# Four transformer layers on one core: order of work chosen per engine, other ranks, corrected costs, second batch begun later

## The reference

```
h = norm(x) * (1 + scale) + shift       # scale, shift, gate from the condition
x = x + gate * self_attention(h) @ Wo   # 16 heads of 16
x = x + gate * cross_attention(norm(x), context) @ Wco
x = x + gate * mlp(norm(x))             # 256 -> 1024 -> 256
```

## Time and profile before

| | |
|---|---|
| median of 3 runs | 3409.06 us (3408.49 to 3410.03) |
| profiled execution | 3412.44 us, span 3410.7 us |
| mean granted TensorE clock | 0.884 |
| TensorE busy | 2778.7 us |
| VectorE busy | 1942.9 us |
| ScalarE busy | 1529.7 us |
| POOL busy | 664.6 us |

### The profile page before, as it was taken

How to read it: one execution, slowest core, us unless ns; L and a number is a source line. 1 busy time by engine, 2 the same in 40 slices (tenths; PEclk the granted TensorE clock), 3 DMA queues, 4 the chain that set the end, 5 groups by cost and what they waited for, 6 DMA issues and landing times.

```text
span 3410.7 us, 44340 instructions
## 1 busy us (share of the span) xinstructions
PE 2778.7 (81%) x13323; PEld 1254.6 (37%) x13376; DVE 1942.9 (57%) x4404; ACT 1529.7 (45%) x2745; POOL 664.6 (19%) x970
## 2 busy tenths in 40 slices
PE   4899999888789898889777655785478989889777
PEld 3423343235325223243443434452223522323335
DVE  6785666332583776634444577338786278745141
ACT  2136546562444665645444223332244265655442
POOL 4011101201410111221141246212431001031020
PEclk8789999899789999989877767897589999999868
DMA  4511112311621322330553333322121031231140
GB/s 155 185 28 45 45 56 77 111 42 42 192 62 41 101 78 67 97 96 20 145 160 90 100 115 107 84 67 86 49 66 34 16 108 50 89 103 39 35 130 23
DMA packets 254273, 275.88 MB, mean 81 GB/s; under 512 B 60485, under 2 KB 195423, under 8 KB 253663
## 3 DMA queue, kind: packets, MB, share of 16 engines
q1 hardware_dynamic: 242783, 271.58, 27.0%
q0 software_dynamic: 11264, 1.46, 0.3%
HBM read 157.36 MB, written 114.09 MB: 80 GB/s over the span
## 4 chain that ended last, share of the span: by engine, by line
PE 62%; DVE 13%; DMA 8%; issue 7%; ACT 5%; POOL 2%; SPq 1%; ACTq 0%; DVEq 0%; POOLq 0%
PE ring_c L1267 10%; PE ring_a L1193 10%; PE ring_b L1237 8%; PE ring_b L1290 7%; PE ring_a L1302 6%; PE ring_b L1152 4%; PE ring_a L1279 3%; PE ring_b L1236 3%; ACT probs L1371 3%; DVE row_max L1533 3%; DMA reciprocals<-scr_recip 2%; PE ring_b L1118 2%; PE ring_a L1290 2%; PE ring_a L1166 1%; PE ring_b L1261 1%
## 5 line engine op out<-in xcount | busy, mean ns | idle before, releaser
L1371 ACT ACTIVATE probs<-ring_b 128x512 f32<-128x512 f32 (+1 forms) x1728 | 910.4, 601 | 691.6 <-PE ring_b L1237 596.1
L1533 DVE TENSOR_REDUCE row_max<-ring_a 128x1 f32<-128x1024 f32 x512 | 599.2, 1219 | 99.8 <-PE ring_a L1193 95.5
L1237 PE MATMUL ring_b<-q_ring,k_ring 100*128 100x512 bf16 x1536 | 525.8, 391 | 85.2 <-ACT probs L1371 61.0
L1193 PE MATMUL ring_a<-k_ring,q_ring 96*128 96x512 bf16 x1536 | 476.5, 403 | 36.1 <-DVE row_max L1533 21.6
L1267 PE MATMUL ring_c<-probs,v_and_ones 128*17 128x512 f32 x3072 | 420.0, 619 | 10.7 <-ACT probs L1371 7.4
L1651 POOL CAST neg_max_parts<-neg_max 16x128 bf16<-16x128 f32 x112 | 33.6, 300 | 1696.5 <-ACT neg_max L1365 1217.3
L1530 DVE CUSTOM_DVE_ANT_0 w_mlp<-ring_a,w_mlp 128x1024 bf16<-128x1024 f32 x256 | 301.3, 1222 | 87.1 <-PE ring_a L1193 86.1
L1577 DVE TENSOR_TENSOR x_tok<-x_tok,ring_a 128x512 f32<-128x512 f32 x96 | 66.0, 687 | 447.1 <-PE ring_a L1302 284.9
L1237 PEld LDWEIGHTS ring_b<-q_ring,k_ring 100*128 100x128 bf16 x1536 | 144.7, 99 | 374.0 <-issue 260.5
L1193 PEld LDWEIGHTS ring_a<-k_ring,q_ring 96*128 96x128 bf16 x1536 | 119.8, 100 | 402.3 <-issue 355.4
L1290 PE MATMUL ring_b<-h_feat,w_mlp 128*128 128x512 f32 x512 | 235.4, 610 | 4.2 <-ACT h_feat L1336 3.4
(11 more groups left out here) (138 smaller groups left out, 3390.2 us busy)
## 6 DMA issues: line engine op xcount, KB each, us to landing
q_ring<-scr_q SPq DMA_DIRECT2D x128, 384.0 KB, 4.0
scr_q<-split SPq DMA_DIRECT2D x64, 384.0 KB, 2.6
k_ring<-scr_k SPq DMA_DIRECT2D x64, 384.0 KB, 5.0
scr_q<-split SPq DMA_DIRECT2D x64, 256.0 KB, 3.0
scr_out<-out_stage SPq DMA_DIRECT2D x128, 128.0 KB, 2.9
scr_out<-out_stage SPq DMA_DIRECT2D x64, 256.0 KB, 2.8
h_feat<-scr_out SPq DMA_DIRECT2D x56, 256.0 KB
reciprocals<-scr_recip SPq DMA_DIRECT2D x56, 256.0 KB
```

What stands on the lines that cost most here:

```text
L1193: last = mm(ps[:, half * BLOCK:(half + 1) * BLOCK], q[0:PARTS, h, t * P:(t + 1) * P], k_view(g)[0:PARTS, h, half * BLOCK:(half + 1) * BLOC ...
L1237: last = mm(ps[:, :], k_view(g)[0:ROWS, h, s.kt * P:(s.kt + 1) * P], q[0:ROWS, h, q0:q0 + BLOCK], start=not g.masked, stop=True)
L1371: f(PT[0:n, s.pt, :], ps[0:n, :], ACT.Exp, **kw).then_inc(b_evac, 1)
L1533: v.tensor_reduce(NM[:, s.nm, s.u:s.u + 1], ps, AX.X, ALU.max).then_inc(a_evac, 1)
```

## The change

`run()` takes the step that can begin first (ties by rank), looks at the engine of its first phase, and picks by rank only among steps that begin on this engine, within a reach that depends on it: PE 0.25 us as before, ACT 5, DVE 0.8, POOL 0.15, SP 2. The ranks change: top-k to 0 and 1, the scores of cross-attention and the context's projections to 0, self-attention's scores to 5 beside its maxima, MLP and products with v to 6, cross maxima and all of window attention to 8. (`init` and `mod` of the table are used by no thread.) A new request `("many", pool, n, free)` takes n places at once when at least `free` are free; scores ask for four, the turns of top-k for two (with four free for the first pair of a unit). Some believed costs change, and the second batch's thread starts at 60 instead of 16 us of the planner's clock.

```diff
@@ -159,6 +159,16 @@
                     t.at = max(t.at, p.since[i])
                     p.uses[i] += 1
                     reply = (i, p.last[i], p.uses[i])
+                elif w[0] == "many":
+                    p = self.pools[w[1]]
+                    if len(p.free) < w[3]:
+                        return False
+                    reply = []
+                    for _ in range(w[2]):
+                        i = p.best()
+                        p.free.remove(i)
+                        t.at = max(t.at, p.since[i])
+                        reply.append((i, p.last[i]))
                 else:
                     if w[1] not in self.flags:
                         return False
@@ -199,8 +209,10 @@
             if not ready:
                 assert not self.threads, [(t.rank, t.send) for t in self.threads]
                 return self
-            first = min(at for at, _ in ready)
-            at, t = min(((at, t) for at, t in ready if at <= first + 0.25), key=lambda x: (x[1].rank, x[0]))
+            first, head = min(((at, t) for at, t in ready), key=lambda x: (x[0], x[1].rank))
+            eng = head.want["ph"][0][0]
+            at, t = min(((at, t) for at, t in ready if t.want["ph"][0][0] == eng and at <= first + REACH[eng]),
+                        key=lambda x: (x[1].rank, x[0]))
             s, t.want = t.want, None
             self.emit(s, at)
             t.at = max(t.at, s["t0"])
@@ -211,7 +223,9 @@
     return Step(kind=kind, ph=ph, after=list(after), counts=list(counts), **kw)
 
 
-RANK = dict(init=0, mod=2, prep=1, out=0, ctx=2, load=1, cross_f=3, cross_s=3, mlp=4, self_f=5, self_pv=5, self_s=6)
+RANK = dict(init=7, mod=0, prep=1, out=0, ctx=0, load=1, cross_f=8, cross_s=0, mlp=6, self_f=5, self_pv=6, self_s=5, tk=0, tk_s=1, win_f=8, win_s=8)
+REACH = dict(PE=0.25, ACT=5, DVE=0.8, POOL=0.15, SP=2)
+DELAY = [8.0, 60.0]
 
 
 def plan():
@@ -274,7 +288,7 @@
                      which=which, hh=hh, blk=blk, raw=raw, raw_last=raw_last, split=sp, sp_uses=sp_uses - 1, width=width,
                      rope=rope, h=h)
         p.raise_flag(("proj",) + key, s)
-        d = yield do("split", ([("PE", 1.0 * (0.6 if ck else 1))] if rope else []) + [("DVE", f * (4.4 if rope else 2.0) + 0.4)],
+        d = yield do("split", ([("PE", 1.0 * (0.6 if ck else 1))] if rope else []) + [("DVE", f * (4.4 if rope else 1.85))],
                      after=[s], ring="a" if rope else None, counts=["split_n"], of=s, rope=rope, l=l)
         p.give("RAW", raw, d)
         w = yield do("scratch", [("SP", 1.5)], after=[d], lat=3.5, of=s, done=d)
@@ -303,11 +317,11 @@
         p.spawn(projections(st, key, whiches), rank("prep"))
         p.spawn(loads(st, key, whiches), rank("load"))
         if topk:
-            p.spawn(topk_units(st, key), rank("cross_f"))
+            p.spawn(topk_units(st, key), rank("tk"))
         else:
-            p.spawn(firsts(st, key), rank("self_f" if kind == "full" else "cross_f"))
-            p.spawn(seconds(st, key), rank("self_s" if kind == "full" else "cross_s"))
-        p.spawn(products(st, key), rank("self_pv" if kind == "full" else "cross_s"))
+            p.spawn(firsts(st, key), rank({"full": "self_f", "window": "win_f", "cross": "cross_f"}[kind]))
+            p.spawn(seconds(st, key), rank({"full": "self_s", "window": "win_s", "cross": "cross_s"}[kind]))
+        p.spawn(products(st, key), rank({"full": "self_pv", "window": "win_s", "cross": "cross_s"}[kind]))
         for hh in range(KF):
             for n in range(hh * st.groups // KF, (hh + 1) * st.groups // KF):
                 yield ("flag", key + ("put", n))
@@ -431,7 +445,7 @@
             row = yield from row_load(l, 0, "vb")
         for blk in range(BLOCKS):
             h = yield ("flag", key + ("h", BLOCKS - 1 if st.akind == "window" else blk))
-            s = yield do("v", [("PE", 4.7), ("DVE", 1.8)], after=[h, w, last, row], ring="a", l=l, b=b, u=blk, last=last, row=row,
+            s = yield do("v", [("PE", 4.4), ("DVE", 1.5)], after=[h, w, last, row], ring="a", l=l, b=b, u=blk, last=last, row=row,
                          h=h)
         if row is not None:
             p.give("ROW", row.slot, s)
@@ -505,8 +519,8 @@
             g = s.g
             for kt in range(TILES if kind == "full" else 1):
                 unit = Step(g=g, kt=kt, last=kind != "full" or kt == TILES - 1, quarter=[], scores=[])
-                for tile in range(4):
-                    qt, pt_last, _ = yield ("get", "PT")
+                places = yield ("many", "PT", 4, 4)
+                for tile, (qt, pt_last) in enumerate(places):
                     pe = 0.43 if (kind == "full" and g.masked) else 0.45 if kind == "window" else 0.22
                     s = yield do("score", [("PE", pe), ("ACT", 0.6)], after=[g.max_put, m, pt_last], ring="b", g=g, kt=kt, fn="exp",
                                  tile=tile, pt=qt, pt_last=pt_last)
@@ -592,19 +606,19 @@
             unit = Step(g=g, kt=0, last=True, quarter=[None] * 4, scores=[])
             for hp in range(2):
                 ts, ts_last, _ = yield ("get", "TS")
-                k = yield do("tk_scores", [("PE", 0.85), ("DVE", 1.0)], after=[g.load, ctx, ts_last], ring="a", g=g, hp=hp, ts=ts,
+                k = yield do("tk_scores", [("PE", 0.85), ("DVE", 0.85)], after=[g.load, ctx, ts_last], ring="a", g=g, hp=hp, ts=ts,
                              ts_last=ts_last)
                 s3, s3_last, _ = yield ("get", "S3")
-                s = yield do("tk_mark", [("DVE", 8.7)], after=[k, s3_last], counts=["tk_n"], of=k, s3=s3, s3_last=s3_last)
-                p.spawn(topk_rest(st, key, g, unit, k, s), (RANK["cross_s"], st.l, st.b, st.blks[0]))
+                s = yield do("tk_mark", [("DVE", 6.0)], after=[k, s3_last], counts=["tk_n"], of=k, s3=s3, s3_last=s3_last)
+                p.spawn(topk_rest(st, key, g, unit, k, s), (RANK["tk_s"], st.l, st.b, st.blks[0]))
             p.give("Q", g.q, k, k.t0 + 0.9)
 
     def topk_rest(st, key, g, unit, k, mark):
-        s = yield do("tk_args", [("POOL", 5.4)], after=[mark], counts=["tkarg_n"], of=k, mark=mark)
+        s = yield do("tk_args", [("POOL", 5.1)], after=[mark], counts=["tkarg_n"], of=k, mark=mark)
         p.give("S3", mark.s3, s)
         e = yield do("tk_exp", [("ACT", 0.75)], after=[s], counts=["tkexp_n"], of=k, arg=s, fn="exp")
-        for h in range(2):
-            qt, pt_last, _ = yield ("get", "PT")
+        places = yield ("many", "PT", 2, 2 if unit.scores else 4)
+        for h, (qt, pt_last) in enumerate(places):
             s = yield do("tk_turn", [("PE", 0.9), ("ACT", 0.6)], after=[e, pt_last], ring="b", of=k, e=e, h=h, pt=qt, pt_last=pt_last)
             unit.quarter[k.hp * 2 + h] = qt
             unit.scores.append(s)
@@ -733,7 +747,7 @@
     p.spawn(contexts(), (2, 0, 0, 0), 30.0)
     p.spawn(rope3(), (3, 0, 0, 0))
     for b in range(BATCH):
-        p.spawn(network(b), (1, 0, b, 0), 8.0 + 8.0 * b)
+        p.spawn(network(b), (1, 0, b, 0), DELAY[b])
     p.run()
     return p
```

## The result

The changed kernel takes 3254.14 us (median of 4 runs, 3244.98 to 3270.32) against 3409.55 in the same comparison: ratio 0.9549, 95% interval 0.951 to 0.9587, 4.5% or some 155 us less. The forecast was 3300 (3205 to 3435). Its profiled execution took 3256.22 us with a span of 3254.4; the one before 3412.44. The amount of work is the same (13376 weight loads of TensorE and 4404 VectorE instructions in both traces; of the 13376 matmuls the trace before holds 13323, the one after 13324).

What follows compares the result with a forecast made beforehand. The kernel was taken as bound by the order in which two batches share the engines, not by one engine. Top-k 59, MLP 35 and start 15 summed to 109 us less: 3300 us, range 3205 to 3435.

Steps and rivals of the forecast that it cites:

- two signs of being wrong: TensorE's idle time not falling below about 540 us, or falling in the passages instead of in top-k and tail.
- Top-k, 59 us: Top-k stretches of both batches: 7 and 32 us from a denser loop, 20 from an earlier first start.
- 16 x 11.4 = 182 us a batch: Top-k loop: sixteen units at the plan's 11.4 us spacing, against 189 us in the first batch and 246 in the second.
- The first top-k could also begin sooner: First top-k: its scores would stand before an MLP block now ahead of them; 20 us gained, ends 0 and 34.
- MLP behind self-attention, 35 us: Program's end: batch 1's scores go first, and deferred MLP blocks fill its tail; 35 us gained, ends 0 and 65.
- Second batch later, 15 us: Program's start: shifting batch 1 from 16 to 60 lets batch 0's maxima start sooner; 15 us gained, ends 0 and 30.
- Cross firsts last, 0 us (-20 to +120): Cross-attention's maxima yield the shared `ring_a` slots to self-attention's; no cost, as the other batch's attention covers it.
- Rival B: Layers 1 and 3, batch 0: cross firsts, now last, starve cross-attention; 3491 us, or 3410 to 3450; chance 0.18.
- Wider reach, 0 us: Lower-ranked steps placed before they are ready hold up their engine's queue; taken as 0, ends 0 and +40 us.
- the 80 us that steps held up behind a waiting one could have cost: VectorE queue: a hundred steps, each holding it for 0.8 us under the wider reach.
- Rival A: Passages between layers fill too with the other batch's MLP; a third of 632 idle us goes, 3200 us; chance 0.15.
- 200 us of idle time there: TensorE's idle time in the two top-k stretches, 1926 to 2115 and 2269 to 2515: 95 + 105 us.

Runs made afterwards that it cites:

- e11: Changed kernel with top-k at rank 3 again instead of 0 and 1: 3287.6 us, ratio 0.9653.
- e1: Changed kernel with the five corrected believed costs put back to their old values: 3340.6 us, ratio 0.9779.
- e7: Kernel before with only the new rule of choice and its reach: 3371.6 us, ratio 0.9894.
- e2: Changed kernel with the old rule of choice, lowest rank within 0.25 us on whatever engine: 3400.2 us, ratio 0.9964.
- e8: Kernel before with self-attention's scores at 5, products at 6, places taken four at once, two for top-k: 3385.6 us, ratio 0.9938.
- e10: Changed kernel with cross-attention's maxima at rank 3 again instead of 8: 3284.2 us, ratio 0.9641.
- e12: Changed kernel with a reach of 0.25 us on every engine, choice still within one engine: 3270.4 us, ratio 0.96.
- e4: Changed kernel with self-attention's products at 5 and scores at 6, as before: 3408.0 us, ratio 0.9982.
- e9: Changed kernel with all ranks of before except self-attention's scores at 5 and products at 6: 3319.6 us, ratio 0.9746.
- e6: Changed kernel with LINK, the planner's believed time between engines, 0.14 instead of 0.15 us: 3269.0 us, ratio 0.9588.
- e5: Changed kernel with LINK, the planner's believed time between engines, 0.16 instead of 0.15 us: 3252.1 us, ratio 0.9545.
- e3: Changed kernel with all ranks of before: 3372.0 us, ratio 0.988.

## Why the prediction was right or wrong

The time, 3254 against 3300, is inside the range and on the forecast side; 155 us were gained where 109 were forecast. What the argument began with held: the kernel is bound by the order, the work is the same, and the gain is idle time (129 us) and 27.5 us less of TensorE's busy time, in part the clock. But most terms of the sum rest on a wrong mechanism, and their total was right partly by chance. Of its own two signs of being wrong, one did not come: the idle time is 503 us, below 540. The other came in part: the idle time was to fall in top-k and tail, and it fell by 40 us in top-k but not in the tail (from batch 1's last maximum to the end 65 us before, 64 after), while the largest part, 54 us, fell in the self-attentions, which the sum did not name. The 7 us that it took as what can be told were also too few: runs of the changed kernel lie 25 us apart, and two nudges 17.

- **Top-k, 59 us.** The stretch did lose 58 us and 40 of its idle time, but not by a denser loop: "16 x 11.4 = 182 us a batch" failed, since the halves took 211 and 314 us, and it is the gap of 154 us between them that went. The rank is worth 35 us (e11), where the order of blocks is what changes, a mechanism the prediction did not have. The costs are worth 78 (e1), and none of it as a shorter top-k: e1's copies span 499 us, the changed kernel's 531. "The first top-k could also begin sooner", 20 us, failed too: it begins at 1924.9, as before, although batch 1 was 142 us ahead there (its layer 1 ends at 1780 instead of 1922), because batch 0's window attention ends 72 us later (1890 instead of 1818). It now shares TensorE with batch 1's cross-attention and MLP of layer 1; its own rank of 8 is not the cause, since at 3 the order is the same.
- **MLP behind self-attention, 35 us.** The edit that this rested on does not exist: the variable is not used. What it foresaw at the end did happen, for another reason. Batch 1's self-attention ends 214 us sooner (3027 against 3241) and its last 227 us hold 183 us of TensorE, both batches' MLP blocks among them, where 170 held 129; its last 168 us alone hold 139 (129 before), as the prediction asked. Of the 214, 58 are taken back by the longer end.
- **Second batch later, 15 us.** The edit does nothing. The first maximum did move, from 162 to 107. The rule of choice does it alone (107.8 in e7), but it is not needed for most of it: e2, which has the new ranks and costs and the old rule, stands at 117, and e8, which has only scores first of all this, at 163.7. At 200 us of TensorE's work done the changed kernel was some 17 us ahead, about the size that was forecast; the prediction had taken the right effect from the wrong line.
- **Cross firsts last, 0 us (-20 to +120).** Worth 31 us of gain, outside the range on its good side: e10. Rival B, starvation, fell; the place where it was looked for, layer 1's cross maxima, moved by 16 us (first one at 1416 instead of 1399.5).
- **Wider reach, 0 us.** 17 us of gain, no harm: right within noise, and the 80 us that steps held up behind a waiting one could have cost appear nowhere. But the same paragraph passed over the choice within one engine. Its absence costs 124 us, the 141 of e2, which takes back both, less the 17 of e12.
- **Self-attention's scores before its products: not in the sum at all.** The step that failed is this omission. The two numbers stood in the diff, and they separate the length of self-attention in all fourteen kernels: where scores go first batch 1's of layer 1 takes 326 to 392 us, where products go first 448 to 476. Before, its scores had rank 6, against 5 for self-attention's maxima and products and 1 for the other batch's preparation and MLP. In 1560 to 1704, with all maxima done, TensorE was busy for 119 us, and 19 of them were these scores (L1237); among the rest were one of batch 0's MLP blocks and its projections. That late scores also hold up the maxima, because a group's key slot comes free only with its last score, was read from the code and not tested by itself; the maxima of batch 1's layer 1 do take 325 us before and 316 in e4, against 232 in the changed kernel and 199 in e8. The row of L1371, 596 us of ScalarE waiting for L1237, was on the page and was not read.

Rival A (the passages fill too) holds in part. From batch 1's output projection to the end of its layer 1 TensorE idles for 30 of 234 us, where it was 50 of 218. But 33 idle us stand between there and top-k, in a stretch of 145 us that before lasted 4, so that up to top-k the passage has gained nothing.

What stays open is why the parts need each other. Scores first without the choice per engine gives 21 us, with it, the costs and the other ranks 155. e2 is the plain case: its self-attention is short (376 and 372) and the time is lost elsewhere, batch 1's last MLP of layer 0 ending 95 us later (1172 against 1077) with 43 us more of TensorE's busy time over the program (2794.5 against 2751.2) and 99 more of its idle time. Which early choice does that was not traced. The request for four places was not tried alone: without it the planner, under the new ranks, finds no step to place at some point. Nor was the single buffer of marks tested, since a second does not fit beside the other tiles. The new ranks of cross-attention's scores (0) and of the context (0) were not taken back by themselves either, and they are an open rival for a share of e9's 67 us: in the planner's own time, which ends at 3307 us for the changed kernel, cross scores at 3 end at 3418.

This time, which `plan()` gives to its last step without a chip, already held most of the table. For the ten kernels with the new believed costs it is 3307 us in the changed one, 3321, 3327 and 3327 in e6, e5 and e12, 3353 and 3354 in e11 and e10, 3414 in e9, 3466 in e2, 3507 in e3 and 3518 in e4. The chip's times have the same order within the size of a nudge, but for e2 and e3. So most of what an undo costs is already lost in the plan, and does not first appear on the chip.

## What to carry to other kernels

In a scheduler with priorities, the first thing to read is which stream has the longest chain behind it; here it is the scores that feed ScalarE's exponentials, and with the rest of the change in place two swapped numbers decided 148 us; by themselves, on the kernel before, they gave 21. Check that each edited number reaches the program before giving it a price: compare the order that comes out, since three edits of this change alter nothing. And when every undo loses most of a gain, nudge a number without meaning before believing in either a cause or luck.

## What the runs showed that was not expected

The top-k stretch gained without a denser loop. The prediction's 200 us of idle time there left out the 154 us between the two halves, which held 31 more; from first copy to last it was 231, and it is 191 in the changed kernel. What changed there is that batch 1 arrives earlier, so that its half follows batch 0's without a gap. And with the same 5254 steps TensorE's busy time varied by some 40 us between orders. Records that are missing from a trace are not the reason: the traces of e5 and e2 both hold all 13376 matmuls, and they have 2755.9 and 2794.5 us, with a mean granted clock of 0.888 and 0.878.
